# Two FFNs of a four-layer block: down projection two tiles behind the up projection, and the wait for the squares' buffer behind the copy of h

## The reference, cut to what matters

```python
def _ternary_linear(x, w):
    alpha = jnp.mean(jnp.abs(w))
    w_t = jnp.sign(w) * (jnp.abs(w) > 0.5 * alpha).astype(w.dtype)
    rms = jnp.sqrt(jnp.sum(x * x, axis=-1, keepdims=True)) / jnp.sqrt(d)
    return jnp.einsum('bsd,fd->bsf', x / (rms + EPS), w_t)
h = jax.nn.gelu(_ternary_linear(layernorm(x), w_up), approximate=False)   # 256 -> 1024
x = x + _ternary_linear(h, w_down)                                        # 1024 -> 256
```

## Time and profile before

| | us |
|---|---|
| median of 3 runs | 2365.93 |
| lowest and highest | 2363.47, 2369.75 |
| the profiled execution | 2368.05 |
| its span | 2366.3 |

### The profile page before, as it was taken

How to read it: one execution, slowest core, us unless ns; L and a number is a source line. 1 busy time by engine, 2 the same in 40 slices (tenths; PEclk the granted TensorE clock), 3 DMA queues, 4 the chain that set the end, 5 groups by cost and what they waited for, 6 DMA issues and landing times.

```text
span 2366.3 us, 47628 instructions
## 1 busy us (share of the span) xinstructions
PE 1824.5 (77%) x12321; PEld 1478.2 (62%) x12321; DVE 2117.0 (89%) x9102; ACT 1656.0 (70%) x5481; POOL 956.6 (40%) x1608
## 2 busy tenths in 40 slices
PE   5888888788888777877777788877877877343887
PEld 3555555455587666777777777777766777342654
DVE  6888777679817999999999999999999999999887
ACT  4878888667746666667777777777777666555776
POOL 0000000001005666666665666666666555666110
PEclk8999899889997888788888777888778777666999
DMA  6000000000000000000000000000000000000001
GB/s 189 18 18 22 18 18 18 13 1 1 1 1 1 1 1 1 1 1 1 2 1 1 1 1 2 1 1 1 1 1 1 1 1 1 1 1 1 10 28 36
DMA packets 14351, 25.00 MB, mean 11 GB/s; under 512 B 1280, under 2 KB 12032, under 8 KB 13824
## 3 DMA queue, kind: packets, MB, share of 16 engines
q1 hardware_dynamic: 14080, 21.97, 3.2%
HBM read 12.27 MB, written 4.19 MB: 7 GB/s over the span
## 4 chain that ended last, share of the span: by engine, by line
DVE 63%; PE 14%; issue 13%; ACT 5%; POOL 0%; DVEq 0%; POOLq 0%; ACTq 0%
DVE xs L1581 9%; DVE pn L1561 8%; DVE bank L1565 8%; DVE U L1630 7%; DVE bank L1595 7%; DVE pn L1586 6%; DVE kv L1619 5%; PE bank L282 3%; PE bank L267 3%; ACT prob L923 2%; PE bank L585 2%; DVE bank L1603 2%; DVE bank L1615 1%; PE bank L632 1%; PE bank L669 1%
## 5 line engine op out<-in xcount | busy, mean ns | idle before, releaser
L750 PE MATMUL bank<-U,ident 128*128 128x128 f32 x2048 | 463.5, 398 | 159.6 <-ACT go L1064 140.1
L750 PEld LDWEIGHTS bank<-U,ident 128*128 128x128 f32 x2048 | 430.1, 257 | 195.5 <-issue 162.3
L1779 POOL TENSOR_TENSOR wu<-U,stg 128x256 f32<-128x256 f32 x512 | 317.7, 620 | 561.3 <-DVE U L1630 561.3
L1253 ACT ACTIVATE xs<-U 128x128 f32<-128x128 f32 x1024 | 261.4, 301 | 304.1 <-DVE U L1630 301.4
L761 PE MATMUL bank<-stack,tm 128*128 128x64 f32 x1792 | 273.8, 324 | 110.1 <-ACT tm L994 100.4
L761 PEld LDWEIGHTS bank<-stack,tm 128*128 128x128 f32 x1792 | 263.7, 237 | 127.5 <-ACT tm L994 115.8
L1708 POOL TENSOR_TENSOR kv<-stg 128x256 f32<-128x256 f32 x513 | 317.4, 619 | 0.0
L1581 DVE TENSOR_TENSOR xs<-U,bank 128x128 f32<-128x128 f32 x1024 | 243.5, 278 | 62.1 <-ACT bank L1107 61.1
L1565 DVE TENSOR_TENSOR bank<-wu,bank 128x128 f32<-128x128 f32 x1024 | 290.0, 283 | 1.8 <-POOL wu L1779 1.4
L735 PE MATMUL bank<-wcat,yT 128*128 128x224 f32 x1024 | 275.9, 425 | 5.8 <-issue 5.4
L1595 DVE TENSOR_TENSOR bank<-pn,bank 128x128 f32<-128x128 f32 x1024 | 248.3, 288 | 1.1 <-issue 0.8
(11 more groups left out here) (213 smaller groups left out, 3708.0 us busy)
## 6 DMA issues: line engine op xcount, KB each, us to landing
out_x<-x SPq DMA_DIRECT2D x8, 512.0 KB, 2.9
x<-in_x SPq DMA_DIRECT2D x1, 3584.0 KB, 16.9
Vs<-V SPq DMA_DIRECT2D x8, 384.0 KB, 4.6
Vs<-V SPq DMA_DIRECT2D x8, 288.0 KB, 3.3
lane<-in_lanes SPq DMA_DIRECT2D x8, 256.0 KB, 3.2
wcat<-in_wcat SPq DMA_DIRECT2D x1, 1792.0 KB, 14.5
wraw<-in_w_up SPq DMA_DIRECT2D x1, 1024.0 KB, 19.0
wraw<-in_w_down SPq DMA_DIRECT2D x1, 1024.0 KB, 11.4
```

The source lines that it names most:

```text
L750: last = pe.matmul(rsum.rearrange("p (t i) -> p t i", i=HD), ident[:, :], steps[:, :, :, j], start=(j == 0), stop=(j == HD - 1))
L1779: pool.tensor_tensor(ij(wu[:, :]), ij(U[:, half if j else 1 - half, (j - 1) % STEPS, :]), col(stg[:, half, j, TW, :]), ALU.mult).then_inc( ...
```

## The change

`hh` gets a third buffer, and its index is t % 3 in place of t % 2 for ScalarE, VectorE and TensorE. TensorE's down follows the up two tiles behind instead of one, and the last two tiles' downs are issued at the end. ScalarE's copy waits for down of tile t-3 instead of t-2. The wait for the squares' buffer moves from ahead of the copy to between the copy and the square. No instruction with data is added or taken away.

```diff
-        hh = sb("hh", [P, 2, 2, L], F16, mid)
+        hh = sb("hh", [P, 3, 2, L], F16, mid)
...
-                                         hh[:, t % 2, part, u * P:(u + 1) * P], wdn[:, e, :],
+                                         hh[:, t % 3, part, u * P:(u + 1) * P], wdn[:, e, :],
...
                 for n in range(NF):
                     up(q, n)
-                    if q > i * B or n > 0:
-                        down(q * NF + n - 1)
+                    if q > i * B or n > 1:
+                        down(q * NF + n - 2)
                     if n == 1 and q > i * B:
                         square_sums(q - 1)
                     if n in (2, 3) and q < i * B + B - 1:
                         turned_rows(pe, q + 1, 3 - n)
-            down((i * B + B) * NF - 1)
+            for t in (2, 1):
+                down((i * B + B) * NF - t)
             square_sums(i * B + B - 1)
...
                     if t >= 2:
-                        act.wait_ge(F["dnm"], t - 1)
+                        act.wait_ge(F["dnm"], t - 2)
+                    act.activation(hh[:, t % 3, 0, :], h[:, t % 2, :], ACT.Copy, scale=HI_H).then_inc(F["hh"], 1)
+                    if t >= 2:
                         act.wait_ge(F["ss"], q * (NF - 1) + max(n - 2, min(n, 2) - 1))
-                    act.activation(hh[:, t % 2, 0, :], h[:, t % 2, :], ACT.Copy, scale=HI_H).then_inc(F["hh"], 1)
                     act.activation(hsq[:, t % 2, :], h[:, t % 2, :], ACT.Square).then_inc(F["sq"], 1)
...
-                    dve.scalar_tensor_tensor(hh[:, t % 2, 1, :], h[:, t % 2, :], HI_H, hh[:, t % 2, 0, :],
+                    dve.scalar_tensor_tensor(hh[:, t % 3, 1, :], h[:, t % 2, :], HI_H, hh[:, t % 3, 0, :],
```

## The result

| | before | changed |
|---|---|---|
| median of 4 runs each, us | 2366.23 | 2342.38 |
| lowest to highest | 2363.47 to 2369.75 | 2340.67 to 2346.68 |
| the profiled execution | 2368.05 | 2343.13 |
| its span | 2366.3 | 2341.3 |

The ratio is 0.9894 with a 95% interval of 0.9874 to 0.9914; the forecast was 2343.5 us.

What follows compares the result with a forecast made beforehand. No engine full, three near it: a loop that waits on itself. Gains of 8.3 us in the first FFN and 14.15 in the second, together 22.4, took 2368.05 to 2345.6, less 2.1 for the median 2343.5; 8-in-10 range 2336 to 2353.

Steps and rivals of the forecast that it cites:

- five steady groups: Groups of 512 rows between an FFN's end groups; each to give back 0.35 us in the first FFN, 1.54 in the second.
- H0: Start of VectorE's low half of a group's tile 0; the second FFN's 1.17 us idle ahead of it was to go.
- H2: Start of VectorE's low half of tile 2; the second FFN's 0.37 us idle ahead of it was to go.
- H3: Start of VectorE's low half of tile 3; 0.16 us idle ahead to go, but paid back ahead of H4.
- H4: Start of VectorE's low half of tile 4; the 0.90 us idle ahead of it was to stay.
- the read: VectorE's read of the previous group's square sums, at n = 2; tile 4's low half was to stay 3.07 us behind it.
- part 2: ScalarE's wait for the squares' buffer moved behind the copy; price alone 0 to 0.5 us, taken as 0.2.
- part 1: TensorE's down two tiles behind up, with three buffers of hh; no instruction added, the low half gets one more tile of time.
- B: Rival: the stall ahead of tile 4's low half goes too, 12 us more, 34 in all, 2331.5 us; chance 9%.
- C: Rival: a new wait, for normalised rows or the square, takes the old one's place; gain 12 us, 2354; chance 15%.
- D: Rival: TensorE's granted clock falls to 1.2 GHz; slower, 2385 us if a quarter of tiles are hit; chance 3%.
- E: Rival: the stage between the FFNs or scatter takes the gain back, no change seen, within 7 us; chance 5%.

Runs made afterwards that it cites:

- e4: The changed kernel with VectorE's read of the square sums one tile earlier (n = 1 instead of n = 2): 2330.15 us, ratio to before 0.9838.
- e5: The kernel before with only VectorE's read of the square sums one tile earlier: 2368.26 us, ratio to before 0.9996.
- e7: The kernel before with only the third buffer of hh and the copy's later wait: 2366.70 us, ratio to before 1.0004.
- e2: The kernel before with only the wait for the squares' buffer moved behind the copy: 2368.23 us, ratio to before 0.9997.
- e1: The changed kernel with the wait for the squares' buffer ahead of the copy again: 2347.06 us, ratio to before 0.9914.
- e3: The changed kernel with two buffers of hh instead of three, down still two tiles behind: 2350.51 us, ratio to before 0.9922.
- e6: The changed kernel with down three tiles behind, four buffers of hh and square sums one tile later: 2352.06 us, ratio to before 0.9917.
- e8: The changed kernel unaltered, timed and traced again: 2343.08 us, ratio to before 0.9899.

## Why the prediction was right

Point by point, forecast and measured; all are differences in us. The mechanism held. The median came within 1.1 us of the forecast partly by luck: the FFNs gave 2.85 us more than the sum had, and the stages around them, which only scatter, took 1.4 of it back.

| step | forecast | measured |
|---|---|---|
| first FFN, first group | -2.1 | -2.36 |
| first FFN, five steady groups | -1.75 | -2.21 |
| first FFN, seventh | -1.3 | -1.15 |
| first FFN, last | -3.1 | -3.19 |
| second FFN, first group | -2.1 | -3.22 |
| second FFN, five steady groups | -7.7 | -8.63 |
| second FFN, seventh | -2.25 | -2.41 |
| second FFN, last | -2.1 | -2.08 |
| sum | -22.4 | -25.25 |

- **Which stalls go and which stays.** Right: those ahead of H0, H2 and H3 are gone, H4's stays, with 3.06 us from the read. e4 shows that the read is its cause, e5 that before the change the down of tile 2 came next in line, 0.4 us earlier. One reading was off: the 0.25 us at 2254.21 do show TensorE idle in front of ready work, but that work was up (4); down (3) still needed the low half that starts at 2254.26. In the changed kernel both up (4) and down (2) are ready in the 0.95 us ahead of 2257.49, and neither passes.
- **TensorE's order is what held the kernel, not the buffer.** Right: the buffer alone gives nothing (e7), part 2 alone nothing (e2), and with the new order e1 and e3 each keep 20 of 25 us. What "with two it would put the copy behind the down again" costs was named without a number in the prediction; it is 5.0.
- **The steady groups gave more than forecast**, 1.73 for 1.54 in the second FFN. The term was mis-sized: I took the idle ahead of H2 for 0.37. An idle is counted from the end that the trace shows for VectorE's instruction in front, which lies some 0.1 us behind the point where the next can start. H2 moved from 4.83 to 4.36, the read by as much, from 6.70 to 6.22. Ahead of H0 the same holds.
- **The second FFN's first group** gave 3.2 for 2.1. I had put 1 us on TensorE at half clock there, as in the earlier trace rows, and that is the term that did not come. Before the change TensorE issued two ups and then idled 2.73 us in front of the first down; the clock fell to 0.50 half a us behind its start:

```profile
2210.87 1.37 PE L282 MATMUL bank<-wdn,hh 128*128 128x256 f16 x8 [2.73 <-ACT hh L327]
```

In the changed kernel it issues three ups in one go, idles 1.86 us, and the clock stays at 1.00. The rows from its timeline: the three ups, VectorE's first low half, the first down, and the fourth up, which takes 1.03 instead of 1.91:

```profile
2197.66 2.75 PE L267 MATMUL bank<-xh,wup 128*128 128x512 f16 x12
...
2201.49 0.69 DVE L415 SCALAR_TENSOR_TENSOR hh<-h,hh 128x512 f16<-128x512 f32 x1
...
2202.28 1.03 PE L282 MATMUL bank<-wdn,hh 128*128 128x256 f16 x8 [1.86 <-ACT hh L327]
...
2204.63 1.03 PE L267 MATMUL bank<-xh,wup 128*128 128x512 f16 x4
```

- **The last groups** were walked to 12.1 and 12.85 and took 12.02 and 12.88. Their first and last low half in the second FFN of the changed kernel, answering to the earlier trace rows:

```profile
2319.06 0.68 DVE L415 SCALAR_TENSOR_TENSOR hh<-h,hh 128x512 f16<-128x512 f32 x1
...
2331.94 0.68 DVE L415 SCALAR_TENSOR_TENSOR hh<-h,hh 128x512 f16<-128x512 f32 x1
```

- **Part 2** was the weak place. I gave the wait a price of 0.2 in its new place and never said what it would have cost in its old one. It is 5.1 us (e1), and nothing without part 1 (e2): the sooner the copy could start, the more it stood on that wait. "A little more" was the wrong size.
- **Rivals.** B did not come, and e4 turned it into a version. C's waits are there but small: the transposes wait for the normalised rows 4.2 us in all in the first FFN, and the square waits 8.9; neither reaches VectorE in a steady group. D is real but begins a tile further on (e6). E did not come: the stages around the FFNs did not take the gain back; that their scatter is some 4 us each is why 25.25 in the FFNs and 23.85 in the medians agree only roughly.
- **One sign of being wrong was badly chosen.** A stage between the FFNs that changes by more than 3 us was to speak against me, and the first trace has 5.3 more. But the twelve traces spread over 8 us there, and the second trace of the same kernel (e8) has 0.2 more than before. A sign must lie outside the scatter, and I had not measured it.

## What to carry to other kernels

When an in-order engine alternates between a producer's and a consumer's work, walk one period with starts of instructions on each engine and ask of each idle which wait ended last; what a lag of one more tile frees is the idles on the loop, and an idle that hangs on a fixed chain from another point stays until that point moves. An edit can be worth nothing alone and 5 us behind another one, so price a wait in the new schedule, in its old place and in its new one. And stop adding lag when the engine's single idle gets long: here the next tile of lag gained nothing and let TensorE's clock fall.

## What the runs showed of the hardware

The same code outside the FFNs scatters by some 4 us to either side of its middle, while the sum of the FFNs' lengths repeats to 0.1 us in the same kernel (272.97 and 273.00, 261.15 and 261.08) and lies within 0.3 us in three kernels with the same order (298.22, 298.39 and 298.44). A pass of VectorE over 128 x 512 fp32 elements shows 0.69 us, and the next starts 0.60 behind it (2251.03 and 2251.63 in the changed kernel), so an idle read from the shown end is some 0.1 us too short.

The granted clock stayed at 1.00 through idles of TensorE up to 1.4 us in the steady groups of the changed kernel, through 1.65 us in e1, through 1.86 us ahead of 2202.28 in the changed kernel, and through 1.91 us ahead of 530.22 in e6. It fell to 0.50 in or behind idles of 2.26, 1.92, 2.31 and 3.73 us in e6 and 2.73 us in the kernel before. The length of the one idle does not say when it falls: at 549.90 it fell inside an idle of 2.26 us, while at 589.11 it stood at 1.00 through the whole of 2.31 us and fell only about 1.4 us after it, with TensorE at work.
